# Codebook FFN after a four-layer mixer on one core: which rows GpSimd gathers, in what order, with which waits, and how many lookups stand ahead of the main loop

## The reference

```python
x = layernorm(x + mixer(x))        # Win 512->64, 4 layers of (silu, complex decay scan, 64->256->64 FFN), Wout 64->512
Wg = codebook[idx_gate].reshape(1376, 512)   # codebook: 8192 rows of 8 floats
Wu = codebook[idx_up].reshape(1376, 512)
Wd = codebook[idx_down].reshape(512, 1376)
x = layernorm(x + (silu(x @ Wg.T) * (x @ Wu.T)) @ Wd.T)
```

## Time and profile before

| | |
|---|---|
| median of three runs | 1306.84 us |
| the profiled execution's own time | 1303.51 us |
| its span, first to last instruction | 1301.5 us |
| TensorE (PE) busy | 1241.4 us, 95% |
| VectorE (DVE) busy | 1052.6 us, 81% |
| GpSimd (POOL) busy | 850.0 us, 65% |
| ScalarE (ACT) busy | 262.4 us, 20% |
| mean granted TensorE clock | 0.981 |

### The profile page before, as it was taken

How to read it: one execution, slowest core, us unless ns; L and a number is a source line. 1 busy time by engine, 2 the same in 40 slices (tenths; PEclk the granted TensorE clock), 3 DMA queues, 4 the chain that set the end, 5 groups by cost and what they waited for, 6 DMA issues and landing times.

```text
span 1301.5 us, 16670 instructions
## 1 busy us (share of the span) xinstructions
PE 1241.4 (95%) x5467; PEld 864.9 (66%) x5467; DVE 1052.6 (81%) x2290; ACT 262.4 (20%) x395; POOL 850.0 (65%) x815
## 2 busy tenths in 40 slices
PE   6868999979999999999999999999999999999998
PEld 4534444436777777777777777776777776778876
DVE  3998999868988778878778878777878777879845
ACT  2325676674000000000000000000000000000025
POOL 3566656666677777777766777566777666777700
PEclk8978999989999999999999999999999999999999
DMA  9322222201334323343323433323333323334303
GB/s 216 55 68 52 59 51 52 51 3 36 97 94 93 68 69 87 90 92 83 71 59 84 92 87 83 73 61 76 92 89 84 71 60 78 90 76 87 67 1 130
DMA packets 97291, 98.54 MB, mean 76 GB/s; under 512 B 50797, under 2 KB 55669, under 8 KB 97206
## 3 DMA queue, kind: packets, MB, share of 16 engines
q1 hardware_dynamic: 67572, 89.16, 23.6%
q0 software_dynamic: 25600, 3.33, 7.7%
q10 hardware_dynamic: 4034, 4.98, 1.3%
HBM read 92.50 MB, written 4.90 MB: 75 GB/s over the span
## 4 chain that ended last, share of the span: by engine, by line
PE 87%; DVE 8%; issue 2%; ACT 1%; SPq 1%; DMA 1%; DVEq 0%; ACTq 0%
PE cand L684 46%; PE bank L684 40%; DVE one_hot L1076 3%; DVE work L1060 1%; DMA book_in<-in_L_ffn_codebook 1%; DVE small L1060 1%; DVE chosen L1094 1%; PE cand L860 1%; SPq L325 0%; ACT x L537 0%; PE bank L951 0%; DVE x L1060 0%; DVE tab L1060 0%; ACT x1t_hi L541 0%; DVE work L1321 0%
## 5 line engine op out<-in xcount | busy, mean ns | idle before, releaser
L428 POOL DMA_INDIRECT stage_down<-in_L_ffn_codebook,idx_down x688 | 726.9, 1057 | 335.9 <-issue 185.3
L684 PE MATMUL cand<-one_hot,book 128*128 128x512 f32 (+1 forms) x2592 | 665.7, 399 | 17.1 <-DVE one_hot L1076 17.1
L1076 DVE TENSOR_SCALAR one_hot<-bc,low_of 128x512 fp32r<-128x512 uint16 (+1 forms) x1296 | 545.3, 482 | 116.7 <-PE cand L684 114.6
L684 PEld LDWEIGHTS cand<-one_hot,book 128*128 128x128 f32 x2592 | 477.8, 189 | 206.4 <-issue 61.8
L1094 DVE SCALAR_TENSOR_TENSOR chosen<-bc,high_of,cand 128x512 f32<-128x512 uint16 (+1 forms) x324 | 235.1, 726 | 10.8 <-PE bank L684 7.5
L684 PE MATMUL bank<-x1t_hi,w 128*128 128x512 f32 (+1 forms) x704 | 242.0, 399 | 0.0
L415 POOL DMA_INDIRECT stage_up<-in_L_ffn_codebook,idx_up x112 | 121.0, 1080 | 51.0 <-issue 30.4
L684 PEld LDWEIGHTS bank<-x1t_hi,w 128*128 128x128 f32 (+1 forms) x704 | 130.2, 185 | 33.2 <-issue 2.1
L684 PE MATMUL bank<-x1t_lo,w 128*128 128x512 f32 (+1 forms) x352 | 138.8, 394 | 0.0
L630 ACT ACTIVATE prod<-bank 128x512 f32<-128x512 f32 (+1 forms) x44 | 26.3, 598 | 390.7 <-PE bank L684 390.7
L637 ACT ACTIVATE act_hi<-prod 128x512 fp32r<-128x512 f32 x40 | 25.3, 632 | 335.4 <-DVE prod L1060 335.4
(11 more groups left out here) (179 smaller groups left out, 755.6 us busy)
## 6 DMA issues: line engine op xcount, KB each, us to landing
bc<-index_parts SPq DMA_DIRECT2D x292, 256.0 KB, 3.2
stage_down<-in_L_ffn_codebook,idx_down POOLq DMA_INDIRECT x688, 2.8
bc<-index_parts_rest SPq DMA_DIRECT2D x32, 192.0 KB, 3.2
x<-in_L_attn_x ACTq DMA_DIRECT2D x4, 1024.0 KB, 10.8
out_x<-x SPq DMA_DIRECT2D x16, 256.0 KB, 2.0
stage_up<-in_L_ffn_codebook,idx_up POOLq DMA_INDIRECT x112
index_parts<-parts_t SPq DMA_DIRECT2D x20, 32.0 KB, 1.9
w_in<-in_L_attn_W ACTq DMA_DIRECT2D x2, 256.0 KB, 8.4
```

Source lines behind the costliest of these rows:

```text
L428: pool.indirect_dma_start(stage_down[k % RING][:, q, j * CS:(j + 1) * CS], None, a["L0_ffn_codebook"], bass.IndirectOffsetOnAxis(ap=idx_do ...
L684: return pe.matmul(dst, lhs, rhs, start=start, stop=stop)
L1076: done = v.tensor_scalar(one_hot[quad % 2][:, q, 0:nw], bc[quad % BCS][:, 0:nw], low_of[:, q:q + 1], None, ALU.is_equal)
```

## The change

1. `POOLED` is now all ten full up units. Of each, GpSimd gathers one turn (what was called a round) in place of one part: turn 0 of all four parts. Such a unit has turns 1 to 3 of four parts, 12 quads. `turn_up` puts the gathered rows, eight columns at a time, in four places of the bank, with 16 matmuls of 8 output rows in place of 4 of 32.
2. All quads are 312 in place of 324, and the gathers 848 in place of 800 (160 up, 688 down).
3. Items of the mixer have 2 quads and 1 quad by turns, 24 in all; 32 quads stand ahead of the main loop, and each full tile has 28.
4. GpSimd's program is the list `GATHERS`. It waits for no landing and for no step: only until `stage_up` or a `stage_down` buffer is free, and until the indices are there. The gathers of up tile k wait until up tile k-1 is summed.
5. `stage_down` has four buffers. `idx_down` holds five tiles' indices, and SP refills it during the main loop.
6. The indices of the up gathers are copied on VectorE out of the loaded table (`keep_up`), in place of seven DMAs.

The core of the diff:

```diff
-    POOLED = {2 * k + 1: ahead for k, ahead in zip(
-        range(3, FULL), ((3, 0), (5, 3), (6, 2), (7, 1), (8, 0), (8, 3), (9, 2)))}
-    def parts_in(unit):
-        return 3 if unit in POOLED else 4
-    ORDER = [(unit, n, part) for unit in range(2 * TILES) for n in range(ROUNDS) for part in range(parts_in(unit))]
+    TURNS, PARTS = 4, 4
+    POOLED = [2 * k + 1 for k in range(FULL)]
+    GATHERS = "U0 D0 U1 D1 D2 D3 U2 D4 U3 D5 U4 D6 U5 D7 U6 D8 U7 D9 U8 D10 U9".split()
+    def turns_of(unit):
+        return range(1, TURNS) if unit in POOLED else range(TURNS)
+    ORDER = [(unit, turn, part) for unit in range(2 * TILES) for turn in turns_of(unit) for part in range(PARTS)]
...
-    RING = 3
+    RING = 4
+    IRING = RING + 1
-    AHEAD_QUADS = EARLY + 2 * ITEMS
+    AHEAD_QUADS = EARLY + 3 * ITEMS // 2
+    REFILL = 12
     def quads_in(t):
-        return range(EARLY + 2 * t, EARLY + 2 * t + 2)
+        first = EARLY + 3 * (t // 2) + 2 * (t % 2)
+        return range(first, first + 2 - t % 2)
     def quads_of(k):
+        per_tile = (ALL_QUADS - AHEAD_QUADS) // FULL
+        return range(AHEAD_QUADS + per_tile * k, AHEAD_QUADS + per_tile * (k + 1))
...
+            def gather_up(k):
+                pool.wait_ge(s["index_up_kept"], 1 if k == 0 else 2)
+                if k:
+                    pool.wait_ge(s["summed"], rounds_through(POOLED[k - 1]))
+                for j in range(JD):
+                    pool.indirect_dma_start(stage_up[:, j * CS:(j + 1) * CS], ...).then_inc(s["up_in"], 16)
+            def gather_down(k):
+                pool.wait_ge(s["index_down_in"], 16 * (1 + max(0, k - RING)))
+                if k >= RING:
+                    pool.wait_ge(s["turned_down"], k - RING + 1)
+                for q in range(KT):
+                    for j in range(JD if k < FULL else REST // CS):
+                        pool.indirect_dma_start(stage_down[k % RING][:, q, j * CS:(j + 1) * CS], ...)
...
+            def refill(k):
+                done = k - IRING
+                sp.wait_ge(s[f"down_in{done % RING}"], 16 * KT * JD * (done // RING + 1))
+                sp.wait_ge(s["index_down_in"], 16 * done + 16)
+                sp.dma_start(idx_down[:, :, place:place + columns], idn[:, :, k * JD:k * JD + columns]).then_inc(...)
...
             def turn_up(unit):
-                pe.wait_ge(s["up_in"], 16 * JD * (list(POOLED).index(unit) + 1))
+                pe.wait_ge(s["up_in"], 16 * JD * (POOLED.index(unit) + 1))
                 for q in range(KT):
-                    mm(bank[3 + unit % 2][P - SUB:P, q * P:(q + 1) * P], stage_up[:, q * SUB:(q + 1) * SUB], ident[:, :])
+                    for part in range(PARTS):
+                        column = (PARTS * q + part) * CS
+                        mm(bank[3 + unit % 2][part * SUB:part * SUB + CS, q * P:(q + 1) * P], stage_up[:, column:column + CS], ident[:, :],
+                           False, False)
```

More of the change, by code:

```diff
@@ L140, in round_of, with rounds_through @@
     def round_of(quad):
-        unit, n, _ = ORDER[quad]
-        return ROUNDS * unit + n
+        return quad // PARTS
+    def rounds_through(unit):
+        return sum(len(turns_of(u)) for u in range(unit + 1))
     def ends_round(quad):
-        unit, n, part = ORDER[quad]
-        return part == parts_in(unit) - 1
+        return quad % PARTS == PARTS - 1
     def ends_unit(quad):
-        return 0 <= quad and ends_round(quad) and ORDER[quad][1] == ROUNDS - 1
-    def sums_at(quad):
-        return ends_round(quad - 2)
+        return 0 <= quad and ends_round(quad) and ORDER[quad][1] == TURNS - 1
     def rows_in(unit):
@@ L301, in spread_parts @@
             def spread_parts(quad):
-                unit, turn_n, part = ORDER[quad]
-                n, slot = unit // 2, unit % 2 * UNIT + ROUNDS * part + turn_n
+                unit, turn, part = ORDER[quad]
+                n, slot = unit // 2, unit % 2 * UNIT + TURNS * part + turn
                 nw = width(quad)
@@ L355, in _ @@
             for quad in range(EARLY, ALL_QUADS):
+                for k in range(IRING, TILES):
+                    if quad == quads_of(k - IRING)[REFILL]:
+                        refill(k)
                 spread_parts(quad)
@@ L385, in _ @@
                                pattern=[[HIGH, CS]], channel_multiplier=-1).then_inc(s["masks_made"], 1)
[L386 to L402, removed]
@@ L443, in _ @@
+            for step in GATHERS:
+                if step[0] == "U":
+                    gather_up(int(step[1:]))
+                else:
+                    gather_down(int(step[1:]))
         @block.scalar
@@ L486, in keep_picked @@
                 nw = rows_in(unit)
[L487 removed]
+                act.wait_ge(s["summed"], rounds_through(unit))
                 if unit >= WRING:
@@ L917, in _ @@
             for t in range(ITEMS):
-                quad, second = quads_in(t)
+                quads = quads_in(t)
                 if t % NC:
@@ L931, in _ @@
                     back(t - 3)
-                candidates(quad)
+                candidates(quads[0])
                 if t >= 2:
                     spread(t - 2)
-                candidates(second)
-                add_up(quad - 1)
-                add_up(second - 1)
+                for quad in quads[1:]:
+                    candidates(quad)
+                for quad in quads:
+                    add_up(quad - 1)
             def turn_down(k, n):
@@ L1301, in _ @@
                     add_mixed(t - 1)
-                one_hots(quad + 1)
+                one_hots(quads[0] + 1)
                 v.wait_ge(s["rs1_made"], t + 1)
@@ L1326, in _ @@
                 tt(d, g, tab[:, l, :], ALU.mult).then_inc(s["damped"], 1)
-                choose(quad)
-                one_hots(second + 1)
-                choose(second)
+                choose(quads[0])
+                for quad in quads[1:]:
+                    one_hots(quad + 1)
+                    choose(quad)
             for b in range(2):
```

83 lines of the change are left out of this document (27 added, 56 removed).

## The result

| | before | after |
|---|---|---|
| median | 1306.71 us (4 runs, 1305.21 to 1307.73) | 1403.45 us (4 runs, 1400.80 to 1405.63) |
| ratio | 1 | 1.074, 95% interval 1.0717 to 1.0764 |
| the profiled execution's own time | 1303.51 us | 1404.63 us |
| its span | 1301.5 us | 1402.8 us |
| mean granted TensorE clock | 0.981 | 0.94 |

The change made the kernel 7.4% slower, and the forecast was 1409 us.

The account below looks back on a forecast made before the run. POOL was taken to bound the kernel: restart at 217 us, 768 gathers, U9 landed at 1264, then 139.5 and 0.4 to a span of 1403.6; plus 2.0 own time and 3.3 for the median, 1409 us, range 1350 to 1440.

Parts of the forecast that it names:

- POOL sets the end, by its pitch and its one idle time: Whole kernel: POOL idles about 100 us at U1 until 217, then runs 768 gathers; U9 made at 1261, landed 1264.
- U2 in tile 1: wanted at 472, landed at 519, a wait of 47: Tile 1, slot 25: PE wants U2 at 472; it is made at 516, landed 2.8 us later; PE waits 47 us.
- Waits of about 19 us in tiles 2, 4 and 6, next to none between: Main loop: cycles ending in even tiles take 108.6 us with about 19 of wait, odd ones 110.2, nearly even.
- The clock after a wait, 3 us each: Main-loop cycles: PE needs 3 us more at the low clock after its wait.
- `turn_up` at 0.87 us: Each turn-up's 32 instructions run side by side in four groups of output rows, 0.87 us; one after another 3.5.
- The pitch: POOL's time per gather, issue included: 1.378 us beside working PE, 1.25 while PE and DVE stand still, mean 1.366.
- The last 3.3 us: End of the sum: the runs' median was taken to stand 3.3 us over the profiled execution, making 1405.6 into 1409.
- the mixer's gain, 15.6 us: Mixer: 8 fewer quads at 1.95 us of PE each save 15.6 us, so tile 0 starts at 292 us.
- POOL keeps up: Rival, 4%: POOL keeps pace, PE sets the end at 1280 us; decided at a pitch of 1.19 us.
- Cheaper gathers: Rival, 13%: gathers shorten beside a less dense DVE; pitch 1.25 to 1.30 gives 1327 to 1363 us.
- a full queue: Rival, 6%: without landing waits, making gathers waits for room; at most 1.72 us a gather, 1661 us.
- They held POOL alone: Gather stream: removing the landing waits and steps was costed at nothing, since they held only POOL.

Follow-up runs that it names:

- The new list: Changed kernel with only GpSimd's gather list reordered (U0 D0 D1 D2 U1 D3 U2 ...), the same 848 gathers: 1282.83 us, first chip.
- the run in one group: Against the reordered-list kernel: all 16 turn-up matmuls of a unit written to the bank's first 8 rows, one column group: 1307.22 us.
- the two kernels with the new list: The changed kernel with reordered gathers alone, 1282.83 us, and the same with all of `turn_up` in one group of output rows, 1307.22 us.
- the three without: Changed kernel on the second chip with D1 put before U1 (2205.80 us), two `stage_up` buffers (2092.19 us), or three down buffers (2092.53 us).
- the control: The changed kernel itself, unaltered, on a fourth chip where the kernel before took 1348.10 us: 2184.57 us.
- the four that were: Changed kernel unaltered (2184.57 us), with D1 before U1 (2205.80), with two `stage_up` buffers (2092.19), with three down buffers (2092.53).

## Why the prediction was right, by its steps

- **POOL sets the end, by its pitch and its one idle time.** Right up to U8. The idle time was forecast at about 100 us up to 217 and is 103.35 up to 221.43; the last gather was forecast to end at 1261 and ends at 1258.7. At U9 the forecast still took the time from the landing, 1264; PE came there at 1262.33 without a wait, so from U8 on PE set the time itself. The new list shows the step from the other side: with the idle time filled, the rest of the kernel as it is, the 120 us are gone.
- **U2 in tile 1: wanted at 472, landed at 519, a wait of 47.** The wait began at 473.4 and ended at 522.50, after 49.06 us. That the 472 is so near is in part luck: tile 0 began 4 us later than forecast, and PE took 177.3 us from there in place of 180.
- **Waits of about 19 us in tiles 2, 4 and 6, next to none between.** 20.68, 19.35 and 18.11; 2.40, 2.12 and 2.36 between. From U2 to U8 the cycles took 1174.3 - 522.5 = 651.8 us, forecast 656 from 516.
- **The clock after a wait, 3 us each.** Too dear. Behind the four long waits the clock stays low to 525.7, 634.9, 853.4 and 1068.4, which is 3.2, 2.8, 5.3 and 3.4 us, but the forecast added 3 us of time. What it cost is less: `turn_up` and sum take 525.88 - 522.50 = 3.38 us behind the first of them and 1264.18 - 1262.33 = 1.85 at full clock, 1.5 us more; it is 1.3, 1.7 and 1.6 behind the others, and 0.8 more for the quad behind the third.
- **`turn_up` at 0.87 us.** It is 0.88, and the run in one group shows that it would be 3.4 otherwise.
- **The pitch.** Forecast 1.366 in the mean; over all 768 it was 1.351, D1 to D3 took 1.342, the stretch beside a full PE 1.365 and the quiet one 1.235. POOL began 4 us late and ended 2 early, so the two errors made up for each other.
- **The last 3.3 us.** The forecast put the median as far above the profiled execution as it was before. It came out 1.2 us under it (1403.45 against 1404.63). Without this term the forecast is 1405.6.
- **The mis-sized term: the mixer's gain, 15.6 us.** Tile 0's first quad went from 307.47 to 296.12, 11.4 us. The step took 8 x 1.95 us of PE as the gain and noted that DVE gets less back only in words. These rows of after, the first quad of item 3, `mix` of item 4 and the first quad of item 13, show one wait of PE for the mixer's own chain on `work`:

```profile
120.93 2.42 PE L643 MATMUL cand<-one_hot,book 128*128 128x512 f32 x8
...
125.72 1.13 PE L643 MATMUL bank<-work,mix 128*128 128x512 f32 x2 [1.32 <-DVE work L1023]
...
215.31 1.95 PE L643 MATMUL cand<-one_hot,book 128*128 128x512 f32 x6
```

  Five odd items between the first and the last gave 102.12 - 94.38 = 7.7 us, 1.55 each. Over them PE is busy for 10.3 us less (97.85 and 87.53), but it stands 2.6 us longer: it waits 3.3 us in three waits for ACT and 2.2 in two for DVE, and before for neither. The first odd item's missing quad hardly shows (121.13 to 120.93), for that item begins 1.5 us later than before (its first quad 97.76, before 96.28). That is not to be laid to the change: the two kernels with the new list, alike up to there, have it at 97.34 and 99.58. The smaller gain and the later start are also why POOL started again at 221 and not at 217, and why PE alone ends at 1279.3 to 1281.2 us of span and not at 1275.1. The main loop's part was right: in the kernel with the new list it takes 1279.3 - 296.9 = 982.4 us in place of 994.0, a gain of 11.6 where 10.8 was forecast.
- **The rivals.** *POOL keeps up* gave 1280 us and stood on a pitch of 1.19, which did not come; the time was reached all the same, by another order at the old pitch. *Cheaper gathers* and *a full queue* did not come on this chip, nor did POOL pass U1 early.
- **"They held POOL alone", of the landing waits and steps.** Nearly true on the first chip (1307.27 us without them against 1304.71), and not shown in general: on the second chip the one kernel with landing waits, which has the new list too, is 610 to 724 us ahead of the three without. No rival had this, and on the chip of the control the time lies 745 us over the range.

**What stays open.** What differs between the first chip and the other three (1304.71 us against 1348 to 1351 for the kernel before) is not known to me; only that it goes with the stalls. Whether the stalled engines lack instructions, semaphore signals or something else the trace does not show, nor whether they would stall without the profiler's recording. Against the missing pause as the whole cause speaks the kernel before: on the first kind of chip 209 of its gathers stand back to back, its steps holding it for 1.2 us in all, and on the others it loses only 3.3 to 3.6%. Whether its steps hold POOL back there is not known, for it was not traced there. The new list without landing waits was not run on the second kind of chip, nor the kernel before without its waits; by the four that were, I would expect both to stall. Whether two `stage_up` buffers or three down buffers change anything on the first kind of chip was not measured either, for they never ran there.

## What to carry to other kernels

Count a gather at its pitch, issue included, and not at its busy time, and before the sum look where the list has its first wait for another engine: everything that could run ahead belongs in front of it. The same 848 gathers cost 120 us or nothing by their order. And do not take a pause out of a long stream of gathers on the ground that only GpSimd seems to wait there: run such a version on more than one chip first, for on one it cost 2.6 us, and on three others such streams came with a loss of over 700 against the kernel before.

## What the runs showed of the hardware that was not expected

- On three of four chips TensorE, VectorE and ScalarE stood together during a stream of gathers without pauses, beginning some 20 gathers into it and lasting up to 25 us beyond it: in 235 us with 187 gathers PE was busy for 46.63, and two stretches of 75 to 80 us without gathers had it at 67.31 and 77.39. The gathers themselves were no slower there ((177.77/187) + 0.30 = 1.25 us). In the one kernel with pauses for landing every five or six gathers PE was busy for 207.95 us of the same 235. Whether the recording has a part in it is open.
- The kernel before was 3.3 to 3.6% slower on these chips too, in 21 runs on three of them against 21 on the first.
- 32 matmuls with 8 output rows each take 0.87 us over four groups of output rows and 3.4 us in one.
